# Two fp32 units around the router ahead of every expert layer, and layer 1's gates by tanh on all partitions

## The reference

```python
x = x + conv_l(ln_c(x))            # l = 0..3, each another block
t = tokens(x)                      # 1024 tokens of 64 channels
t = t + ffn_l(ln_t(t))
```

```python
logits = xf @ gate_w + gate_b
cw = top 2 of the (soft-maxed) logits, 0 elsewhere     # layer 0 routes by image, not by token
out = sum_e cw[:, e] * (gelu(xf @ W1[e] + b1[e]) @ W2[e] + b2[e])
```

```python
ca = sigmoid(ca_mlp(avg) + ca_mlp(mx));  c = out * ca            # a gate per channel
sa = sigmoid(conv7x7([mean_c(c), max_c(c)]))                     # a gate per pixel
cbam_out = c * sa
non_local = out + attention(q, k, v)
y = tail_w @ concat(cbam_out, non_local) + tail_b
```

## Time and profile before

| | |
|---|---|
| median of 3 runs | 207.29 us (207.29 to 207.3) |
| the profiled execution's own time | 206.68 us |
| its span, first to last instruction | 204.9 us |
| PE busy, share of the span | 193.5 us, 94% |
| DVE, ACT, POOL busy | 124.6, 127.5, 42.5 us |
| mean granted TensorE clock | 0.992 of full speed |
| fillers (L294, the bf16 group of the banks) | 110 matmuls, 29.9 us busy |

### The profile page before, as it was taken

The page is one execution under the profiler, slowest core; times in us unless marked ns, Lnnn a source line. Parts: engine busy times, 40 slices in busy tenths (PEclk is TensorE's granted clock), DMA queues, the critical chain, the costliest instruction groups (busy, mean ns, idle before and its releaser), DMA issues.

```text
span 204.9 us, 3052 instructions
## 1 busy us (share of the span) xinstructions
PE 193.5 (94%) x1104; PEld 91.3 (45%) x1112; DVE 124.6 (61%) x352; ACT 127.5 (62%) x213; POOL 42.5 (21%) x60
## 2 busy tenths in 40 slices
PE   7998999999999998999999999999999997799994
PEld 2654322346976865423222346442234594442221
DVE  0457869966760653781824534496675788578565
ACT  2444788748146673876576560597876675488773
POOL 7761000000000000200994000010840022020470
PEclk9999999999999999999999999999999999799999
DMA  6999400000000000000000000000000000000001
GB/s 219 378 407 406 172 0 2 0 0 3 2 3 0 0 3 0 0 5 0 0 0 0 0 0 3 0 0 0 0 6 0 0 2 3 0 0 0 0 3 51
DMA packets 3119, 8.54 MB, mean 42 GB/s; under 512 B 550, under 2 KB 1072, under 8 KB 2976
## 3 DMA queue, kind: packets, MB, share of 16 engines
q1 hardware_dynamic: 2736, 7.73, 9.8%
q0 software_dynamic: 224, 0.48, 0.6%
q10 hardware_dynamic: 144, 0.13, 0.3%
HBM read 8.08 MB, written 0.26 MB: 41 GB/s over the span
## 4 chain that ended last, share of the span: by engine, by line
PE 78%; DVE 7%; ACT 7%; issue 3%; POOL 2%; POOLq 1%; DVEq 0%; ACTq 0%
PE bank L381 16%; PE banks L294 9%; PE banks L398 8%; PE banks L399 7%; PE banks L574 6%; PE bank L305 5%; PE bank L299 4%; ACT hidden L758 4%; POOL total L1455 2%; PE banks L535 2%; PE banks L516 2%; PE bank L343 2%; PE bank L643 2%; PE bank L499 2%; PE bank L328 2%
## 5 line engine op out<-in xcount | busy, mean ns | idle before, releaser
L758 ACT ACTIVATE hidden<-banks,pack_l 128x1024 f32<-128x1024 f32 (+1 forms) x43 | 44.9, 1052 | 18.8 <-PE banks L399 18.4
L381 PE MATMUL bank<-hidden,w 128*64 128x512 f32 (+1 forms) x160 | 41.5, 596 | 1.3 <-ACT hidden L758 1.3
L294 PE MATMUL banks<-idle_work 128*128 128x512 bf16 x110 | 29.9, 404 | 2.0 <-DVE idle_work L1045 1.2
L398 PE MATMUL banks<-split_x,w_hi 128*128 128x512 f16 x80 | 30.7, 384 | 0.0
L399 PE MATMUL banks<-split_x,w_lo 128*128 128x512 f16 x80 | 30.3, 379 | 0.0
L1446 POOL CAST split_x<-normed 64x256 f16<-64x256 f32 x8 | 3.9, 493 | 99.1 <-DVE normed L927 94.2
L716 ACT ACTIVATE squares<-bank 128x256 f32<-128x256 f32 x18 | 6.9, 383 | 22.8 <-PE bank L299 21.4
L398 PEld LDWEIGHTS banks<-split_x,w_hi 128*128 128x128 f16 x80 | 7.8, 97 | 27.1 <-issue 12.8
L294 PEld LDWEIGHTS banks<-idle_work 128*128 128x128 bf16 x117 | 11.7, 106 | 15.2 <-issue 4.8
L1455 POOL TENSOR_TENSOR total<-total,term 128x512 f32<-128x512 f32 x12 | 17.1, 1423 | 1.9 <-DVE term L1022 1.3
L381 PEld LDWEIGHTS bank<-hidden,w 128*64 128x64 f32 x160 | 7.9, 134 | 17.5 <-issue 12.4
(11 more groups left out here) (316 smaller groups left out, 318.2 us busy)
## 6 DMA issues: line engine op xcount, KB each, us to landing
w_stage<-in_w SPq DMA_DIRECT2D x3, 512.0 KB, 13.5
w_stage<-in_w SPq DMA_DIRECT2D x1, 1024.0 KB, 9.6
conv<-in_conv SPq DMA_DIRECT2D x1, 800.0 KB, 7.7
w<-in_w SPq DMA_DIRECT2D x3, 256.0 KB, 13.7
w<-in_w SPq DMA_DIRECT2D x1, 512.0 KB, 10.4
toeplitz<-in_toeplitz SPq DMA_DIRECT2D x1, 512.0 KB, 11.1
gauss<-in_gauss SPq DMA_DIRECT2D x1, 512.0 KB, 12.6
pack_l<-in_pack_l SPq DMA_DIRECT2D x1, 469.0 KB, 11.8
```

Source lines behind the costliest of these rows:

```text
L294: mm(out, idle_work[:, 0:128], idle_work[:, 0:cols], start=True, stop=True)
L381: last = mm(out[64 * h:64 * h + 64, cut], w2[l][:, (f * NE + e) * CH:(f * NE + e + 1) * CH], hidden[v % 3][:, h * 512 + cut.start:h * 512 ...
L398: mm(out, w1_hi[l][:, at:at + 128], split_x[h][:, :], start=True, stop=False)
L758: last = act(hidden[u % 3][:, cut], both[u % 2][:, cut], ACT.Gelu, bias=P(f"l{l}", "e_b1")[:, e * fc + f:e * fc + f + 1])
```

## The change

- **Experts, PE.** Units 0 and 1 (`STRAIGHT = 2`) are made from the fp32 weights as loaded (`stage[l]`) and the normalised activations: for each half h one fp32 matmul over 64 rows, 128 columns of weights and 512 moving columns. They wait for `ln_out` and for the load alone. From unit 2 on the split products are used, and the waits for the split stand there. The router stands between unit 0 and unit 1. The fillers ahead of unit 0 (eight in layer 0, one in the others) are gone.
- **Experts, ACT.** The first Gelu is whole. The tanh of the routing in layers 1 to 3 comes after it. In layer 0 the tanh come before Gelu 0, and after Gelu 2 and Gelu 3, each after the copy of an expert's output that stands there.
- **Routing, DVE.** The low parts are made chunk by chunk. The first of the two maxima is found by one instruction (compare with zero, times rank) on the shifted logits in place of two.
- **Layer 1's gates.** A sigmoid is (1 + tanh(a/2)) / 2. For the channel gate: tanh from PSUM on ACT and one multiply-add on DVE. For the spatial gate: the logits are made for all 128 partitions by eight matmuls with 64 columns of broadcast weights, tanh on ACT from PSUM, and (tanh + 1) times the gated values on DVE; the factor 1/2 goes into the tail's weights, by POOL in its setup. The clamps, ln, and the matmul that spreads the map are gone. The table set ACT loads there is another.
- **Layer 1's order.** A third of chunk 0's attention stands where the first spreading matmul stood; the tail takes the gated input first for both chunks; DVE gates chunk 1 before it normalises chunk 1's attention; the norm's average of chunk 0 comes before the centring of chunk 1.

```diff
-                busy(1 if l else 8, bank[0][:, :])
-                pe.wait_ge(S[f"w1_split{l}"], 2)
-                pe.wait_ge(S[f"w2_loaded{l}"], 16)
+                def up_straight(u):
+                    e, f = divmod(u, fc)
+                    at = e * HIDDEN[l] + f * 128
+                    if u == 0:
+                        pe.wait_ge(S["ln_out"], 2 * k + 2)
+                    for h in range(HALVES):
+                        r = slice(64 * h, 64 * h + 64)
+                        last = mm(both[u % 2][:, h * 512:(h + 1) * 512], stage[l][r, at:at + 128], normed[k][r, :],
+                                  start=True, stop=True)
+                    last.then_inc(S["moe_hidden"], 1)
...
+                pe.wait_ge(S[f"w1_loaded{l}"], 16)
                 for u in range(units):
...
+                    (up_straight if u < STRAIGHT else up_split)(u)
+                    if u == 0:
+                        router()
+                    if u == 1:
+                        pe.wait_ge(S[f"w2_loaded{l}"], 16)
                     wides(u, False)
                     if u:
                         down(u - 1)
...
-                        at = 8 * j + 4 * c + 2 * n
-                        last = mm(gate_ps[j][0:2, 0:PIX], sa_feat[:, at:at + 2],
-                                  toeplitz[:, (2 * c + n) * PIX:(2 * c + n + 1) * PIX],
-                                  start=c + n == 0, stop=c + n == 2)
+                        for h in range(HALVES):
+                            at = 8 * j + 4 * c + 2 * n + h
+                            last = mm(gate_ps[j][64 * h:64 * h + 64, 0:PIX], sa_feat[:, at:at + 1].broadcast_to([128, CH]),
+                                      toeplitz[:, (2 * c + n) * PIX:(2 * c + n + 1) * PIX],
+                                      start=c + n == 0, stop=c + n == 2)
...
             attend(0, range(2))
             queries_keys(1)
             channel_hidden(1)
-            spatial_map(0)
+            attend(0, range(2, 3))
             channel_gates(1)
-            attend(0, range(2, 4))
+            attend(0, range(3, 4))
...
             attend(1)
             center(4, 0, x[3], x_ready(3))
-            spatial_map(1)
             tail(1)
+            average(4, 0)
             center(4, 1, x[3], x_ready(3))
-            averages(4)
+            average(4, 1)
+            busy(NORM_TAIL[4], bank[0][:, :])
...
-                    by_halves = l and u == 0
...
+                    sc.wait_ge(S["moe_hidden"], base + u + 1)
+                    act(hidden[u % 3][:, :], both[u % 2][:, :], ACT.Gelu,
+                        bias=P(f"l{l}", "e_b1")[:, e * fc + f:e * fc + f + 1]).then_inc(S["moe_gelu"], 1)
+                    if l:
+                        between(u)
                     e = u // fc - 1
                     if u and u % fc == 0 and (l == 0 or e < NE - 2):
                         sc.wait_ge(S["moe_y"], base + u)
                         act(y_sb[e], bank[4 + e % 2][:, :], ACT.Identity, bias=P(f"l{l}", "e_b2")[:, e:e + 1])\
                             .then_inc(S["moe_y_sb"], 1)
+                    if l == 0:
+                        between(u)
...
-                if u in (-1, 1, 3):
-                    n = (-1, 1, 3).index(u)
+                if u in (-1, 2, 3):
+                    n = (-1, 2, 3).index(u)
...
-                st.link(TT(g8(c("eq")), g8(values), spread_to(peak, 8), ALU.is_equal))
-                st.link(TT(c("r"), c("eq"), rank[:, 0:n], ALU.mult))
+                st.link(STT(c("r"), below, 0.0, rank[:, 0:n], ALU.is_equal, ALU.mult))
...
-                st.link(TS(gate[2], gate[1], 1.0, None, ALU.add))
-                st.link(V.reciprocal(gate[3], gate[2]))
-                TS(chunk(gated, j), chunk(O, j), gate[3], None, ALU.mult).then_inc(S["gated_c"], 1)
+                st.link(TS(gate, tanh, 0.5, 0.5, ALU.mult, ALU.add))
+                TS(chunk(gated, j), chunk(O, j), gate, None, ALU.mult).then_inc(S["gated_c"], 1)
...
+                ve.wait_ge(S["sa_map"], j + 1)
+                STT(chunk(cbam, j), chunk(sa, j), 1.0, chunk(gated, j), ALU.add, ALU.mult).then_inc(S["cbam_done"], 1)
...
+            setup.link(G.tensor_scalar(P("l1", "tail0"), P("l1", "tail0"), 0.5, None, ALU.mult))
```

More of the change, by code:

```diff
@@ L323, in experts, with router @@
                 fc, base = fc_of[l], unit_base[l]
-                if l:
-                    pe.wait_ge(S["ln_out"], 2 * k + 2)
+                units = NE * fc
+                def router():
+                    if l == 0:
+                        pe.wait_ge(S["ones_set"], 1)
+                        pe.wait_ge(S["routed"], 2)
+                        mm(bank[7][:, 0:INNER * 16], ones[:, :], routed[:, :], start=True, stop=True)\
+                            .then_inc(S["route_logits0"], 1)
+                        return
                     pe.wait_ge(S[f"l{l}_loaded"], 16)
@@ L544, in tail @@
                 pairs = [("tail0", "cbam_done", cbam), ("tail1", "nonlocal_in", nonlocal_)]
-                for n, (weight, ready, src) in enumerate(pairs if j == 0 else pairs[::-1]):
+                for n, (weight, ready, src) in enumerate(pairs):
                     pe.wait_ge(S[ready], j + 1)
@@ L837, in gate_pixels @@
             def gate_pixels(j):
-                part = [sa[:, (4 * j + n) * PIX:(4 * j + n + 1) * PIX] for n in range(4)]
-                sc.wait_ge(S["sa_cl"], j + 1)
-                st.link(act(part[1], part[0], ACT.Exp, scale=-1.0))
-                st.link(act(part[2], part[1], ACT.Ln, bias=P("first", "one")[0:2, :]))
-                act(part[3], part[2], ACT.Exp, scale=-1.0).then_inc(S["sa_map"], 1)
+                sc.wait_ge(S["sa_ps"], j + 1)
+                tanh_half(chunk(sa, j), gate_ps[j][:, 0:PIX]).then_inc(S["sa_map"], 1)
             for j in range(INNER):
@@ L1089, in _ @@
             TT(c4("shifted"), c4("logit"), spread_to(s4("peak"), 8), ALU.subtract).then_inc(S["l0_exp_in"], 1)
-            split(1, 0)
+            for j in range(INNER):
+                split_low(1, 0, j)
             ve.wait_ge(S["l0_exp"], 1)
```

123 lines of the change are left out of this document (45 added, 78 removed).

## The result

| | before | after |
|---|---|---|
| median of 4 runs each, on one chip | 207.29 us (206.53 to 207.3) | 203.83 us (203.39 to 204.22) |
| ratio, 95% interval | | 0.9841 (0.9808 to 0.9874) |
| the profiled execution's own time | 206.68 us | 204.11 us |
| its span | 204.9 us | 202.3 us |
| mean granted TensorE clock | 0.992 | 1.0 |

What follows compares the result with a forecast made beforehand. TensorE, with 78% of the chain that ended last, was taken to bound the kernel, DVE layer 0's end. Gains of 0.55 + 0.18 + 1.05 = 1.78 us off 207.29 gave 205.5 us; 8-in-10 range 204.0 to 206.9.

Steps and rivals of the forecast that it cites:

- The signs of all parts: Gains were forecast for layer 0 (0.55 us), layer 1's convolution stage (0.18) and the heads of layers 1 to 3 (1.05).
- the fall of the clock: Rival, chance 0.10: the lower clock in layer 3's convolution goes, 1.2 us off its path, giving 204.3 us.
- the spatial pair: Layer 1's spatial logits: 0.54 us a pair, 2.16 for four, so 0.34 us more, twice; bounds 0.43 and 0.86 a pair.
- gain of the heads: Expert heads of layers 1 to 3: first down product 0.35 us earlier a layer, 1.05 us for three.
- DVE holds layer 0: Layer 0: first down product 1.4 us earlier, but DVE's routing and sums let only 0.55 through; bounds 0 and 0.7.
- the term of the straight unit: Units 0 and 1 of a head: 1.0 us of PE each, between 0.89 (full overlap) and 1.78 (none).
- the lower bound of 0.89: A straight unit's cost if its two matmuls over 64 rows and 512 columns overlap fully.
- the change of tiling: Two added changes a head between array halves and whole array: 0.12 us each, taken as already held in 1.0 a unit.
- the slack at the transposes: Layers 2 and 3: 0.4 us of slack spent exactly, PE coming 0.35 us earlier and the routing's parts 0.05 later.
- The spatial gates: Layer 1's convolution stage: 0.18 us gained, bounds -2.4 and +1.06.
- The rival in which pairs cost one matmul: Rival, chance 0.10: 0.43 us a spatial pair, 0.89 a straight unit; convolution stage gains 1.06, each head 0.45; 204.3 us.

Runs made afterwards that it cites:

- e7: The changed kernel with layer 0's router ahead of unit 0 and its three tanh ahead of the copies of the experts' outputs; 203.24 us over 10 runs (0.9871).
- f4: The changed kernel with, in layers 1 to 3, the router behind unit 1 and ACT's first tanh behind the second Gelu; 205.46 us over 8 runs.
- e6: The changed kernel with one straight unit instead of two in layers 1 to 3; 203.40 us over 4 runs.
- e3: The kernel before, unaltered, profiled a second time; 205.08 us over 10 runs (0.999).
- e1: The kernel before with the experts' part of the change alone, layer 1's old gates kept; 204.93 us over 10 runs (0.9935).
- the filled ones: The kernel before with six fillers in layer 3's convolution; 205.56 us median over 24 runs.
- e2: The kernel before with the gates by tanh on all partitions and the old heads of the experts; 205.11 us over 10 runs (0.9949).
- e8: e7 with the subtraction that makes the low part of the convolution weights moved from DVE to GpSimd; 205.95 us over 10 runs.
- e4: The changed kernel with seven more fillers behind layer 1's experts, delaying all that follows; 205.63 us over 10 runs.
- f1: The changed kernel with the edits of e7 and e6 together; 202.39 us over 6 runs (0.9827).
- e5: The changed kernel unaltered, run again; 203.20 us over 6 runs (0.9861).
- the changed kernel's first and third: The changed kernel unaltered, in its first batch (203.83 us over 4 runs) and its third; 203.54 us median over all its 20 runs.
- f3: The kernel before with six fillers in layer 3's convolution; 205.56 us median over 24 runs, a second batch of the same included.
- f2: f1 with six fillers added in layer 3's convolution; 202.52 us over 6 runs.

## Why the prediction was wrong, point by point

The measured 203.83 us lie 1.67 below the forecast and 0.17 below the range's lower end. The signs of all parts were right. Two steps failed above all: the sum put the fall of the clock at nothing, where one execution with it was taken for the kernel (1.0 us), and the spatial pair was priced at 0.54 us, where it takes 0.43 (0.8 us). The overpriced gain of the heads (1.05 against 0.61 us) hid part of it. In the order of the prediction:

**What bounds the kernel, and that DVE holds layer 0.** Right. PE gained 1.29 us at layer 0's first down product and DVE let 0.44 through (0.55 forecast). The missing 0.11 lies in the routing chain: the sums start 0.24 later by the second chunk, 0.13 were forecast. e7, which shortens only that chain, confirms it.

**The heads, 1.05 forecast, 0.61 measured.** The mechanism was right (PE decides, T+3.0 to 3.1 forecast, T+3.31 measured), the term of the straight unit was short: 1.06 and not 1.0. It consists of 0.85 for the pair, below the lower bound of 0.89 (f4), and 0.21 for the change of tiling behind it, where the prediction put 0.12 and took it for held in its 1.0. The unit's 0.06 counts twice a head, the first one starts at T+0.13 instead of T+0.05, and the chain puts the down product at T+3.31, 0.07 later than the timeline. The Trainium skill, TensorEngine Tiling (Array Packing), section Key Properties, says that such a change drains TensorE, and f4 agrees with it and gives the price, for which the prediction had only a bound from shapes in a row. That the slack at the transposes would be spent was right in sum and wrong in its parts: PE came 0.18 us earlier and not 0.35, the routing's parts 0.23 later and not 0.05. It caps the head: e6 gains 0.17 in each head and keeps it only in layer 1.

**The spatial gates, 0.18 forecast, 0.98 measured.** This is the largest wrong term of the change itself. The pair was priced at 0.54, from four matmuls in 1.08 us. That row is two pairs with an end in it, which may be why; eight matmuls in a row take 1.73, 0.43 a pair. The chain has the gain where the prediction had a loss, ahead of chunk 1's attention (0.76 of the 0.80 us). The rival in which pairs cost one matmul had this stage at 1.06, and it was right (0.98); it was right too for a straight pair (0.85), but for the heads the changes of tiling took that back. Its chance of 0.10 was too low, and it should have been two rivals: the 64-row matmuls, five steps in 2.09 us, already spoke for the pairs.

**The fall of the clock, 0 forecast, about 1.0 measured.** It was a rival, at 0.10, with 1.2 us; the stage shows 1.0. The sum rested on one profiled execution, and it happened to have the fall. So had, to judge by their times above 206.5, all four runs that the result is measured against, where only runs with a fall lie; none of the changed kernel's 20 has one. The prediction took the median shown as the kernel's time, while it was one of two levels.

**What is left.** 2.03 and 1.0 make 3.03 of the 3.46 us. The rest, 0.4, goes with the start: the second chunk of layer 0's norm ends anywhere from 19.2 to 20.6 us in these profiles, with the same instructions ahead of it. The timelines of the kernel before, and of e3, the same kernel, show where:

```profile
1.19 4.82 PE L294 MATMUL banks<-idle_work 128*128 128x512 bf16 x11 [1.19 <-DVE idle_work L1045]
5.85 1.03 PE L299 MATMUL bank<-x_in,pack_first 128*128 128x256 f32 x4
```

```profile
1.19 4.28 PE L294 MATMUL banks<-idle_work 128*128 128x512 bf16 x11 [1.19 <-DVE idle_work L1045]
5.31 1.03 PE L299 MATMUL bank<-x_in,pack_first 128*128 128x256 f32 x4
```

From the end of this first centring (6.88 and 6.34; 7.27 in the changed kernel, 6.00 in e1) to the second chunk it is 13.20 or 13.21 us in all four. So the whole difference lies in TensorE's first matmuls: the fillers take up to 0.63 us each there and 0.38 from some moment on, which differs between executions (the clock column reads 1.00 in both parts). The kernel's runs with a fall seem to start late: their median less the fall's 1.0 is 205.89, against 205.10 in the runs without and 205.56 in the filled ones, where both kinds are mixed; the one traced with a fall had its second chunk at 20.08, the one without at 19.54. That is no general rule, for e1 and f4 had their fall with the earliest starts of all (19.21, 19.17). That the four runs of before had a late start is therefore argued and was not traced in them.

**What stays open.** Why the changed kernel never met a fall in 20 runs, while e1 (7 of 10), e2 (6 of 10), e8 (7 of 10), e4 (4 of 10), e7 (3 of 10), f4 (1 of 8) and f1 (1 of 6) did, whose thin stretch is the same but lies elsewhere in time. e4 excludes the time since the start as the only cause.

The traces show what goes with it. Their records of the clock, from which the stretches' granted clock is worked out, have its first rise at 5.83 us in the kernel before, 4.05 in e1, 4.83 in e2, 7.09 in e7, 6.16 in e8 and 3.99 in f4. In these six, which are all the traces with the fall, it starts 170.67 us behind the rise (167.25 in e7), and 0.01 to 0.78 us behind the start of the second mixing product, so right behind PE's idle 0.98 us. In e4, e5 and e6, without fillers and without a fall, the moment 170.67 us behind the rise lies 1.56 to 1.63 us behind the start of that product, and the moment 167.25 us behind it 1.79 to 1.86 us ahead of it. In f3 the first of these lies 0.50 us behind it, as in the traces with a fall; there the fillers stand, and the clock did not fall.

So an execution seems to have a fall where PE's thin stretch lies just ahead of a moment fixed by the first rise, and the rise differs from run to run. This is read from ten traces and was not tested: the changed kernel's first and third, e3, f1 and f2 have no record of the rise, and no run moves it on purpose. The Trainium skill, TensorE: Matmul & The Clock Gate, section What's actually happening, calls the window over which activity is judged free-running, so that its phase may differ from run to run. The traces agree: the rise lies anywhere from 3.99 to 7.17 us, and the fall keeps its distance from it.

## What to carry to other kernels

Before a median of a few runs is taken as a kernel's time, look whether the granted clock falls somewhere in the profile: such a fall can be there in half of the runs, and a few fillers in the thin stretch of TensorE take it out at no cost. Price a packed matmul from a long group of its own shape, and charge each change between whole-array and half-array matmuls by itself (0.2 us here). Where an engine gets a microsecond at the head of a stage, follow who releases the stage's last step; here a routing chain on DVE kept 0.85 of 1.29 us in layer 0 and all of a further 0.17 us in layers 2 and 3.

## What the runs showed of the hardware

- A change of tiling behind a pair of fp32 matmuls in row halves costs 0.21 us: 3.11 us for unit, router, unit against 2.91 for unit, unit, router.
- Two fp32 matmuls in two halves cost one: 0.43 us a pair at 256 columns in column halves (1.73 for four), 0.85 us a pair at 512 columns in row halves.
- The fall of the clock to 1.2 GHz in one stretch costs its stage 1.0 us and is present in 54 of 111 runs of one and the same kernel; with PE busy 1.87 instead of 0.67 of 2 us there, in 0 of 24.
- In all six traces with the fall it starts 170.67 us (once 167.25) behind the first rise of the clock, and 0.01 to 0.78 us behind PE's idle 0.98 us.
- The start varies between executions of the same program: the same step of layer 0 is done at 19.61, 20.28 and 20.48 us in three of the changed kernel's, at 19.17 to 20.62 over all kernels traced, by how long TensorE's first matmuls take 0.63 instead of 0.38 us.
- A GpSimd operation of 3.21 us held a DVE operation of 0.19 us with two SBUF inputs for 2.45 us, to its own end.
